# First layer's feed-forward block: two arrangements of value rows, another slot order, and the band mask added by VectorE

## The reference

```python
def shift_tokens(t):
    a, s = jnp.split(t, 2, -1)
    s = jnp.pad(s, ((0, 0), (1, 0), (0, 0)))[:, :-1]
    return jnp.concatenate([a, s], -1)
...
    q = l2norm(q) * qs
    k = l2norm(k) * ksc
    ...
    q = q * cos * scale + rotate_half(q) * sin * scale
    k = k * cos * inv + rotate_half(k) * sin * inv
    out = local_attention(q, k, v)      # 16 heads of 64, windows of 32 rows, each looks at its own and the window before
    return out @ Wo
...
    xn = (x - mu) / jnp.sqrt(var + 1e-05) * g + bln
    a, gate = jnp.split(xn @ W1 + b1, 2, -1)
    return a * jax.nn.gelu(gate, approximate=False) @ W2 + b2
```

## Time and profile before

| | us |
|---|---|
| median of 3 runs | 5369.28 |
| lowest, highest | 5364.82, 5372.76 |
| the profiled execution, its own time | 5376.34 |
| the profiled execution, its span | 5374.4 |
| PE busy in the span | 4459.1 (83%) |
| DVE busy | 3578.9 (67%) |
| ACT busy | 2725.0 (51%) |
| POOL busy | 2494.3 (46%) |

### The profile page before, as it was taken

One profiled execution on the slowest core, in us unless ns is written; L12 is line 12 of the kernel. 1 busy time (PEld: TensorE's weight loads), 2 busy tenths in 40 slices (PEclk: granted clock), 3 DMA queues, 4 the chain that ended last, 5 costly groups with the idle time before them and its releaser, 6 DMA issues. The chain is left out here.

```text
span 5374.4 us, 115360 instructions
## 1 busy us (share of the span) xinstructions
PE 4459.1 (83%) x45624; PEld 2769.2 (52%) x45624; DVE 3578.9 (67%) x6837; ACT 2725.0 (51%) x4622; POOL 2494.3 (46%) x2314
## 2 busy tenths in 40 slices
PE   7768999999999999777863888887798869985779
PEld 5555666666666666524641343433365444423445
DVE  4347777777777777466446999999855526646646
ACT  3325666666666666463323566565465415542322
POOL 8426666666666666343054666666633310001100
PEclk8779999999999999877856999999999959996889
DMA  1001111111111111000000000000000000003000
GB/s 23 16 21 34 30 49 34 46 34 42 38 44 40 30 30 34 17 0 2 2 11 14 1 1 0 1 0 1 3 13 1 1 18 5 16 1 74 5 21 7
DMA packets 110461, 102.56 MB, mean 19 GB/s; under 512 B 37143, under 2 KB 80424, under 8 KB 109160
## 3 DMA queue, kind: packets, MB, share of 16 engines
q1 hardware_dynamic: 107879, 94.14, 7.1%
q0 software_dynamic: 2048, 1.05, 0.1%
HBM read 40.18 MB, written 1.18 MB: 8 GB/s over the span
## 5 line engine op out<-in xcount | busy, mean ns | idle before, releaser
L4201 POOL TENSOR_TENSOR l_attn_read<-l_attn_state,l_attn_c_rows 128x1024 f32<-128x1024 f32 x256 | 605.0, 2364 | 291.0 <-DVE l_attn_state L4103 173.0
L2999 POOL TENSOR_TENSOR l_ffn_t<-l_ffn_t 128x512 f32<-128x512 f32 x384 | 488.3, 1272 | 506.5 <-DVE l_ffn_t L2866 506.5
L2597 PE MATMUL psum<-l_ffn_wq,l_ffn_xsT 128*128 128x512 f32 x1152 | 601.8, 614 | 97.9 <-DVE l_ffn_t L2866 96.5
L3823 PE MATMUL psum<-l_attn_read,ident 128*128 128x512 f32 x1024 | 491.5, 598 | 7.3 <-DVE l_attn_yz L4111 5.0
L3005 POOL TENSOR_TENSOR l_ffn_t<-l_ffn_t,l_ffn_ss 128x512 f32<-128x512 f32 x384 | 401.1, 1045 | 0.7 <-DVE l_ffn_ss L2881 0.7
L2862 DVE TENSOR_TENSOR l_ffn_t<-psum,l_ffn_tab 128x512 f32<-128x512 f32 x384 | 258.8, 674 | 121.9 <-ACT l_ffn_sq L2748 119.2
L4103 DVE TENSOR_TENSOR_SCAN l_attn_state<-l_attn_decay,psum 128x1024 f32<-128x1024 f32 x144 | 329.0, 2284 | 4.5
L2645 PEld LDWEIGHTS psum<-l_ffn_pT,l_ffn_v 64*64 64x64 f32 x3072 | 248.9, 135 | 142.9 <-issue 138.8
L2597 PEld LDWEIGHTS psum<-l_ffn_wq,l_ffn_xsT 128*128 128x128 f32 x1152 | 180.0, 191 | 274.3 <-DVE l_ffn_t L2866 237.7
L3979 ACT ACTIVATE l_attn_decay<-l_attn_dt,l_attn_a 128x1016 f32<-128x1016 f32 x256 | 292.9, 1144 | 36.0 <-DVE l_attn_state L4100 32.6
L2645 PE MATMUL psum<-l_ffn_pT,l_ffn_v 64*64 64x64 f32 (+1 forms) x3072 | 306.1, 227 | 1.1 <-ACT l_ffn_pT L2764 1.1
(11 more groups left out here) (914 smaller groups left out, 11451.6 us busy)
## 6 DMA issues: line engine op xcount, KB each, us to landing
l_ffn_vx<-l_ffn_v SPq DMA_DIRECT2D x192, 128.0 KB
l_ffn_vx<-l_ffn_v SPq DMA_DIRECT2D x384, 64.0 KB
l_ffn_wq<-in_L_ffn_Wqkv SPq DMA_DIRECT2D x6, 1536.0 KB, 6.4
l_xattn_toep<-s4d_taps SPq DMA_DIRECT2D x4, 2048.0 KB, 17.2
l_ffn_wo<-in_L_ffn_Wo SPq DMA_DIRECT2D x6, 512.0 KB, 3.6
l_ffn_w<-in_L_ffn_W SPq DMA_DIRECT2D x6, 341.0 KB
l_ffn_w<-in_L_ffn_w SPq DMA_DIRECT2D x3, 512.0 KB, 4.1
x_all<-in_x SPq DMA_DIRECT2D x4, 256.0 KB, 4.4
```

Source lines behind the costliest of these rows:

```text
L2597: nc.tensor.matmul(ring[it % 2], xsT[:, n % 2, m % G, :], w, start=True, stop=True).then_inc(itemed, 1)
L2999: nc.gpsimd.tensor_tensor(t1[:, m % G, i, :], t1[:, m % G, i, :], t2[:, x % 3, :], ALU.add).then_inc(added, 1)
L3823: last = nc.tensor.matmul(total[:, h * GT:(h + 1) * GT], K.ident[:], read[:, k % 3, h * GT:(h + 1) * GT], start=(n == 0), stop=(n == N - 1 ...
L4201: nc.gpsimd.tensor_tensor(read[:, k % 3, :].rearrange("p (h n) -> p h n", h=2), state[:, k % 3, :].rearrange("p (h n) -> p h n", h=2), row ...
```

## The change

In `l0_ffn`:

- **Value rows.** The arrangement `mixed` is no longer made: two transfers for each `m` in place of six. The third window's weights stand twice in `pT`, once with only the even and once with only the odd pairs of windows kept (`keep` is a column of ones and zeros), so `value` runs two products for each head and side (96 and 64 columns) in place of three (64, 32 and 32), the second adding onto the first. `move_p` becomes three ACT instructions (256, 128 and 256 columns) in place of one of 512.
- **Mask.** PE no longer writes the mask into PSUM ahead of the scores. DVE adds it as it takes the scores out into `p` (one more instruction of 512 columns), and maximum and subtraction then read `p` in SBUF. The next `score` waits for that first instruction (`masked`) and not for the subtraction.
- **Shift.** Only the shifted half of the features goes through PE (one product of 256 columns in place of two); POOL copies the other half (`unshifted_in`).
- **Slot order.** PE: the q or k item first in each slot, the v item last in the odd slots. ACT: `square` first, `exp` last in the even slot, behind `move_turn`. DVE: `add_out` and `total` first, then `rotate`, then `peak`, then `length`. POOL: `scale` ahead of `weigh`. Feed-forward part: `turn_h` at 10, gates at 11, 13, 14, `gelu` at 15, the products `a` with `gated` at 0 to 2 and `down` at 3 of the next step, `moments` at 6.

In `l0_attn`: POOL makes no taps ahead of the first group's root, then three, three and two.

```diff
                 for g in range(NG):
                     if local and g:
-                        s4d.taps(pool, 2 * g)
-                        s4d.taps(pool, 2 * g + 1)
-                    if local and g == 0:
-                        s4d.taps(pool, 0)
-                        s4d.taps(pool, 1)
+                        for a in range(3 * (g - 1), min(3 * g, s4d.HI)):
+                            s4d.taps(pool, a)
...
-                    for par in range(2):
-                        nc.tensor.matmul(S[:, par], K.ident16[:], rows(band16[:], 4), start=True, stop=False, skip_group_check=True)
...
-                        for at, n, kinds in ((0, 2 * W, (own[0], far)), (2 * W, W, (mixed, mixed)), (3 * W, W, (far, own[1]))):
+                        for to, at, n, kinds in ((0, 0, 3 * W, (own[0], far)), (2 * W, 3 * W, 2 * W, (far, own[1]))):
...
-                    nc.tensor.matmul(ps[:, :, 0:64], K.ident[:], r_all[:, q * G:(q + 1) * G, 0:64], start=True, stop=True)
...
@@ block.tensor
                     k = 16 * (tau - 1) + u
+                    if tau < NSTEP:
+                        project(4 * tau + u // 4, u % 4)
                     if k % 2 == 0 and 0 <= k // 2 < NU:
                         score(k // 2)
                     if k % 2 == 0 and 0 <= k // 2 - 1 < NU:
                         turn_p(k // 2 - 1)
-                    if tau < NSTEP:
-                        for i in items_at(u % 4):
-                            project(4 * tau + u // 4, i)
                     if k % 2 == 1 and 0 <= (k - 3) // 2 < NU:
                         value((k - 3) // 2)
                     if turn_at(tau, u) is not None:
                         turn_item(*turn_at(tau, u))
+                    if tau < NSTEP and u % 2 == 1:
+                        project(4 * tau + u // 4, 4 + u % 4 // 2)
                     if out_at(tau, u) is not None:
                         project_out(out_at(tau, u))
...
@@ block.scalar
-                    nc.scalar.copy(pT[:], TP.rearrange("p (h t) -> p h t", h=4)).then_inc(pt_moved, 1)
+                    nc.scalar.activation(to[:, :, 0:4:3, :], blocks[:, :, 0:3:2, :], ACT.Identity, scale=keep[:, 0:1])
+                    nc.scalar.activation(to[:, :, 2, :], blocks[:, :, 2, :], ACT.Identity, scale=keep[:, 1:2])
+                    nc.scalar.copy(to[:, :, 1:5:3, :], blocks[:, :, 1:4:2, :]).then_inc(pt_moved, 1)
...
+                    if tau < NSTEP:
+                        square(4 * tau + u // 4, u % 4)
                     if k % 2 == 0 and 0 <= k // 2 - 1 < NU:
                         move_p(k // 2 - 1)
-                    if tau < NSTEP:
-                        square(4 * tau + u // 4, u % 4)
-                    if k % 2 == 0 and 0 <= k // 2 < NU:
-                        exp(k // 2)
                     if k % 2 == 1 and 0 <= (k - 3) // 2 < NU:
                         move_o((k - 3) // 2)
                     if turn_at(tau, u) is not None:
                         move_turn(*turn_at(tau, u))
+                    if k % 2 == 0 and 0 <= k // 2 < NU:
+                        exp(k // 2)
...
@@ block.vector
-                    nc.vector.reduce_max(mx[:, k % 2, :, :], S, AX).then_inc(max_found, 1)
...
+                    nc.vector.tensor_tensor(by_head, S, band[:].unsqueeze(1).unsqueeze(1).to_broadcast([128, 2, 4, 2 * W]), ALU.add).then_inc(masked, 1)
+                    dve.wait_ge(masked, k + 1)
+                    nc.vector.reduce_max(mx[:, k % 2, :, :], by_head, AX).then_inc(max_found, 1)
...
-                    if k % 2 == 0 and 0 <= k // 2 < NU:
-                        peak(k // 2)
+                    if out_at(*before) is not None:
+                        add_out(out_at(*before))
                     if k % 2 == 1 and 0 <= k // 2 < NU:
                         total(k // 2)
...
                         rotate(4 * tau + u // 4, u % 4)
+                    if k % 2 == 0 and 0 <= k // 2 < NU:
+                        peak(k // 2)
+                    if tau < NSTEP:
                         length(4 * tau + u // 4, u % 4)
...
@@ block.gpsimd
+                def unshifted_in(n):
+                    if n:
+                        pool.wait_ge(filled, use["ht", n - 1] + 1)
+                    for i in range(G):
+                        wait_moved(pool, "op", 4 * n + i)
+                    nc.gpsimd.tensor_copy(xs[:, :, 0:64], r_all[:, n % NG * G:n % NG * G + G, 0:64]).then_inc(half_in, 1)
```

More of the change, by code:

```diff
@@ L2473, in misc_at @@
                     return ("sh", n)
-                if u == 8:
+                if u == 10:
                     return ("ht", n)
-                if u in (9, 10, 11):
-                    return ("g", n, u - 9)
-                if u in (13, 14, 15):
-                    return ("a", n, u - 13)
-            if u == 0 and 0 <= n - 1 < NSTEP:
-                return ("w2", n - 1)
+                if u in GATE_AT:
+                    return ("g", n, GATE_AT.index(u))
+            if 0 <= n - 1 < NSTEP:
+                if u < 3:
+                    return ("a", n - 1, u)
+                if u == 3:
+                    return ("w2", n - 1)
             if u == 12 and tau + 1 < NSTEP:
                 return ("x", tau + 1)
-        slots = [(tau, u) for tau in range(NSTEP + 3) for u in range(16) if tau < NSTEP + 2 or u < 1]
+        slots = [(tau, u) for tau in range(NSTEP + 3) for u in range(16) if tau < NSTEP + 2 or u < 4]
         order = [("x", 0)]
@@ L2545, in spread_v @@
                     for par in range(2):
-                        own, far, mixed = v[:, b, par, :, :], vx[:, m % 2, 0, :, :], vx[:, m % 2, 1, :, :]
+                        own, far = v[:, b, par, :, :], vx[:, m % 2, :, :]
                         at = 2 * W * par
                         sp.dma_start(far[at:at + 2 * W], own[2 * W - at:4 * W - at]).then_inc(spread[m % 2], 16)
-                        sp.dma_start(mixed[at:at + W], own[2 * W:3 * W]).then_inc(spread[m % 2], 16)
-                        sp.dma_start(mixed[at + W:at + 2 * W], own[W:2 * W]).then_inc(spread[m % 2], 16)
                 with nc.allow_non_contiguous_dma(reason="small parameter columns"):
@@ L2569, in _ @@
                             fetch_out(l + 1)
-                        if at == 2 and u == 1 and 1 <= l < DEPTH:
+                        if at == 2 and u == 4 and 1 <= l < DEPTH:
                             fetch_net(l)
@@ L2620, in score @@
                                 keys = (keys[:, 0:2], keys[:, 0:2], newer_first(kT, r, m % G, 4 * c + i), keys[:, 2:4])[w]
-                                last = nc.tensor.matmul(S[W * w:W * w + W, par, i, :], qT[r, m % G, 4 * c + i, W * w:W * w + W], keys, start=False, stop=True,
+                                last = nc.tensor.matmul(S[W * w:W * w + W, par, i, :], qT[r, m % G, 4 * c + i, W * w:W * w + W], keys, start=True, stop=True,
                                                         skip_group_check=True)
@@ L2634, in value @@
                     m, c = k // 2, k % 2
-                    own, far, mixed = [v[:, m % NV, par, :, :] for par in range(2)], vx[:, m % 2, 0, :, :], vx[:, m % 2, 1, :, :]
+                    own, far = [v[:, m % NV, par, :, :] for par in range(2)], vx[:, m % 2, :, :]
                     pe.wait_ge(pt_moved, k + 1)
                     if c == 0:
-                        pe.wait_ge(spread[m % 2], 16 * 6 * (m // 2 + 1))
+                        pe.wait_ge(spread[m % 2], 16 * 2 * (m // 2 + 1))
                     if k >= 1:
@@ L2787, in shifted_in @@
                         act.wait_ge(filled, use["ht", n - 1] + 1)
-                    done(nc.scalar.copy(xs[:].rearrange("p g d -> p (g d)"), take("sh", n)), "sh", n)
+                    done(nc.scalar.copy(xs[:, :, 64:128], take("sh", n).rearrange("p (g d) -> p g d", g=G)[:, :, 64:128]), "sh", n)
                 def norm(n):
@@ L2962, in _ @@
                     n = tau - 2
-                    if k % 2 == 0 and 0 <= k // 2 < NU:
-                        peak(k // 2)
+                    before = (tau, u - 1) if u else (tau - 1, 15)
+                    if out_at(*before) is not None:
+                        add_out(out_at(*before))
                     if k % 2 == 1 and 0 <= k // 2 < NU:
@@ L2975, in _ @@
                         invert(tau - 1, 1)
-                    if out_at(tau, u) is not None:
-                        add_out(out_at(tau, u))
                     if u == 12 and tau + 1 < NSTEP:
@@ L2980, in _ @@
                     if 0 <= n < NSTEP:
-                        if u == 5:
+                        if u == 6:
                             moments(n)
-                        if u in (13, 14, 15):
-                            gated(n, u - 13)
-                    if u == 0 and 0 <= n - 1 < NSTEP:
+                    if u < 3 and 0 <= n - 1 < NSTEP:
+                        gated(n - 1, u)
+                    if u == 3 and 0 <= n - 1 < NSTEP:
                         add_down(n - 1)
@@ L2988, in _ @@
                             finish(n - 1 - NSTEP + NG)
```

(13 more changed lines are left out.)

49 lines of the change are left out of this document (27 added, 22 removed).

## The result

The changed kernel takes 5445.24 us (median of 4 runs, 5443.89 to 5462.80), the kernel before 5367.21 us (4 runs, 5364.82 to 5372.76): the ratio is 1.0151, 95% interval 1.0129 to 1.0173, so 78 us slower. The prediction was 5455. The profiled execution had 5444.5 us with a span of 5442.8, 68.4 longer than the 5374.4 before.

What follows compares the result with a forecast made beforehand. It took PE (95% busy) to bound `l0_ffn` before, and a chain through ACT and DVE to take its place in part. -20.6 + 99 + 8 = +86 on 5376.34 gives 5462, the median 7 lower: 5455 us, range 5330 to 5545.

Steps and rivals of the forecast that it cites:

- `l0_attn`: Without taps ahead of POOL's first root, ACT's norm moves up by its whole idle time: -20.6 us, bounds 0 and -21.6.
- the chain: In `l0_ffn`, serial ACT and DVE work from a pair's even item to the next pair's first item: 7.87 us.
- Quiet pair: Slots 4 and 5 of `l0_ffn`, set by the chain at 7.87 us against 7.13 of PE work.
- The mask's addition: DVE's added instruction in `peak` costs 0.70 us on the chain, with nothing on DVE in parallel.
- ACT late at slots 8 and 0: Norm, gelu and root on ACT delay the first square in these slots by 2.0 and 2.35 us.
- Rival 2: ACT is in time at slots 0 and 8, so a step is 75.6 us, total 5356; chance 0.16.
- The exponential's table load: In pairs 8/9 and 0/1 the load begins only after the wait, adding 1.28 us to the chain each time.
- `value` at 0: PE's `value`, with 32 instructions for 48 but 1280 columns for 1024, was taken to change by 0.
- Rival 4: `value` goes by instruction count: -0.5 us in the three PE-bound pairs, -33 us, total 5422; chance 0.10.
- rival 5: PE's clock falls in new holes of 3 to 4 us; at mean 0.9, +75 us, total 5530; chance 0.12.
- The edges: Two `l0_ffn` steps with attention but not all the rest, taken as +4 us each, +8.
- 69.9: PE's work in us for one `l0_ffn` step if it never waited, 5.7 less than 75.57.

Runs made afterwards that it cites:

- Experiment 2: The kernel before with only the new order of the filter taps in `l0_attn`: 5346.72 us, ratio 0.9964.
- experiment 3: The changed kernel with the odd item's `rotate` ahead of `total` on DVE and its `square` ahead of `exp` on ACT: 5372.32 us, ratio 1.0009.
- experiment 4: The changed kernel with the mask written by PE into PSUM again, `score` waiting for the subtraction: 5335.59 us, ratio 0.9943.
- experiment 6: The changed kernel with ACT's square root in slots 8 and 0 moved from ahead of the square to behind `move_turn`: 5381.52 us, ratio 1.0030.
- Experiment 8: The changed kernel with three unused products added on PE at the end of slot 9, ahead of the longest hole: 5411.29 us, ratio 1.0081.
- experiment 1: The changed kernel with the old order of the filter taps put back in `l0_attn`: 5458.69 us, ratio 1.0178.
- Experiment 9: The changed kernel with the odd item first on DVE and ACT, the mask on PE again and the roots behind `move_turn`: 5225.27 us, ratio 0.9728.

## Why the prediction came out right

The total, 5455 for 5445, and most pairs came out as worked out, but three terms were too high and one rival came in part, and these cancelled.

- **`l0_attn`**, -20.6: right. Experiment 2 has -20.2 for it alone.
- **The bound changes from PE to the chain**: right, and shown by experiment 3, which changes only the order. Quiet pair 7.87 forecast, 7.86 measured; `moments` in pair 6/7 9.29 and 9.35.
- **The mask's addition is on the chain**, 0.70: right, 0.71 from 1222.14 to 1222.85. Undone it gives 3.27 a step (experiment 4). What the sum left out was the second bill, by the clock (2.3 a step, below).
- **ACT late at slots 8 and 0**: right. 2.0 and 2.35 forecast, 2.08 and 2.6 measured, and experiment 6 removes it. Rival 2, that ACT is in time, is out.
- **The exponential's table load on the chain**, 1.28 twice a step: wrong as put. It costs the chain nothing, since it runs while ACT waits for the subtraction. In its place the 1.28 no longer covers `invert`, which delays `total` by 0.5 in pair 8/9, and in pair 0/1 `invert` and one `gated` ahead of `total` cost about 1.1. So 8/9 was 0.8 too high, 0/1 right by accident. The Trainium skill (ScalarE: Activation LUTs, What ACT_TABLE_LOAD costs) gives 1283 ns for the load and 1380 more for a drain. The 1.28 agrees; of the 1.38 these rows show nothing, the root starts 1.30 after the start of its load.
- **`value` at 0**: mis-sized. It gains 0.25 in each pair, and with it 0.09 that came from using 1.05 for the item ahead of it: that row stands behind a hole, and behind no hole the step from item to small tiles is 0.96. Together 0.34 in the three pairs where PE is the bound, 1.0 a step. Rival 4 had 0.5 for the first of these, by the count alone, and got half of it. The Trainium skill (TensorEngine Tiling (Array Packing), Instruction Overhead), on which that rival leaned, says that one column costs what 60 do, and not that 96 cost what 60 do. Read so, and with the columns above 60 in full, a head and side went from 64 + 60 + 60 = 184 to 96 + 64 = 160, 13% less: by that page's figure an estimate of 0.2 of the 1.52, near the 0.25 measured. Per head, 12 products take 0.35 (29 ns each) and 8 take 0.28 (35 ns each).
- **The clock, rival 5**: came in part. The rival had holes of 3 to 4 us in two pairs and a clock of 0.9, the sum a clock of 1.00; it was 0.96, with one hole of 2.92 and, in pair 0/1, 1.6 and 0.87. It adds 2.3 to the 78.43 of a full-clock step. Experiment 8 shows that nearly all of it goes when the longest hole is filled; experiment 1 shows that such a hole does not always bring it.
- **The edges**, +8 for the two steps with attention but not all the rest: mis-sized. 22 x (80.75 - 75.57) = 114 is already more than the 110 that `l0_ffn` grew by, so by the forecast's 75.57 they were about -4.

The step: 80.1 - 0.8 - 1.0 + 0.2 (pair 12/13) = 78.5, and the clock's 2.3 makes 80.8, measured 80.75. The span: 86 forecast, less 22 x 1.65 = 36 for the step at full clock, plus 22 x 2.3 = 51 for the clock, less 12 for the edges, less 13 for the early stages beyond the taps and 9 for the late ones, which the change does not touch, is 67; measured 68.4. So the closeness of the total is partly luck: with the clock at 1.00 the same forecast would have been some 60 too high, though still on the right side.

The list of what would be seen held. The gap on DVE ahead of `total` is small, about 0.1 in the rows above, since `length` fills the rest. Two kinds of hole were not on the list: `value` waits 0.6 to 0.7 for `move_p` in pairs 8/9 and 0/1, and in pair 0/1 the product `a` that follows the v item waits for `gated` on DVE:

```profile
1286.84 1.12 PE L2686 MATMUL psum<-xT,l_ffn_w 128*128 128x512 f32 x2 [1.60 <-DVE l_ffn_gel L2935]
```

What PE would take if it never waited was put at 69.9. Experiment 9, with the mask on PE (0.13 more a pair, as the prediction works it out: 0.31 less the 0.18 of the change of tiles) and `value` at its true size (0.34 less a pair), should then need 69.9 + 1.0 - 2.7 = 68.2. It has 70.45, of which 2.2 are waits, start to start against the same stretch without one (1.24 and 0.48 in pair 8/9, 0.34 in pair 6/7, 0.16 between slots 1 and 2), so but for `value` that floor was right.

What stays open: whether the table load in the earlier trace rows begins late because of its wait or for another reason was not tried, nor which part of the slot order of the feed-forward part helps or harms by itself. Experiment 4 bounds it only together with `value`.

## What to carry to other kernels

When a slot's calls are put in another order, follow one bank from the product that fills it to the product that wants it next, and add up every instruction that stands between on each engine. Here two calls in the wrong order cost 73 us and the mask on the same chain 110, the clock's part in both, with no engine more than 75% busy but PE. Work taken off the bounding engine is paid in full if it lands on the chain that releases that engine's bank, and may be paid again if the clock falls behind the hole that it makes. Cost the order first and the work second: the same value rows and feed-forward slots that ended 78 us slower are 145 us faster than the kernel before with the mask back on PE and `rotate`, `exp` and `root` in other places.
